# The last batch through every expert with gates instead of routing, and the tensor engine's work regrouped by tile form

## The reference, cut to what matters

```
w_eff = cos(phases) * w_real - sin(phases) * w_imag
h = conv1d(x, w_eff, taps=16)                 # 735 tokens, 64 -> 64 features
n = layernorm(h)
h = h + softmax((n Wq)(n Wk)^T / 8) n
n = layernorm(h)
logits = n gate_w + gate_b                    # 16 experts
top 2 logits, softmax over the two = two gates per token
expert e:  relu(n w1[e] + b1[e]) w2[e] + b2[e]      # 64 -> 128 -> 64
h = h + layernorm(n + sum of the two picked experts, each times its gate) * gamma + beta
```

## Time and profile before

| | |
|---|---|
| median of the runs | 450.35 us |
| the profiled execution | 450.88 us |
| its span in the trace | 449.1 us |
| PE busy | 335.5 us (75%) |
| vector engine busy | 246.3 us (55%) |
| POOL busy | 198.3 us (44%) |
| ACT busy | 127.2 us (28%) |
| mean granted TensorE clock | 0.795 of 2.4 GHz |

### The profile page before, as it was taken

One profiled execution on the slowest core, in us unless ns is written; L12 is line 12 of the kernel. 1 busy time (PEld: TensorE's weight loads), 2 busy tenths in 40 slices (PEclk: granted clock), 3 DMA queues, 4 the chain that ended last, 5 costly groups with the idle time before them and its releaser, 6 DMA issues.

```text
span 449.1 us, 6811 instructions
## 1 busy us (share of the span) xinstructions
PE 335.5 (75%) x2138; PEld 210.4 (47%) x2138; DVE 246.3 (55%) x985; ACT 127.2 (28%) x245; POOL 198.3 (44%) x241
## 2 busy tenths in 40 slices
PE   3859567868998798979897987987897776377400
PEld 1423324325654555465465445546744665266400
DVE  5357448244626584768586567848553526304305
ACT  2115103513342253235234432532142211021000
POOL 8000001710364545727572755557264726760170
PEclk9968668979698999899899989996569555555555
DMA  4970521140425241344424334323423322341110
GB/s 125 231 214 1 188 68 30 44 136 34 117 74 149 70 121 66 102 137 132 126 69 143 105 106 130 101 78 95 119 91 98 105 83 89 130 121 60 53 26 23
DMA packets 40915, 44.79 MB, mean 100 GB/s; under 512 B 11280, under 2 KB 30256, under 8 KB 40752
## 3 DMA queue, kind: packets, MB, share of 16 engines
q1 hardware_dynamic: 34736, 38.06, 27.9%
q0 software_dynamic: 6144, 6.30, 5.9%
HBM read 28.68 MB, written 15.66 MB: 99 GB/s over the span
## 4 chain that ended last, share of the span: by engine, by line
PE 62%; DVE 10%; DMA 8%; POOL 7%; ACT 7%; issue 6%; POOLq 0%; SPq 0%; ACTq 0%
PE small L962 18%; PE mix L962 14%; PE up L962 11%; PE wide L962 10%; PE mix L1138 5%; POOL x_far L470 5%; ACT hidden L574 4%; DMA xs<-x_far 2%; POOL ysel L481 2%; DVE row_max L727 2%; DMA w_far<-wt 2%; PE wide L1039 2%; PE wide L1007 1%; PE up L1079 1%; DMA x_far<-xn,place 1%
## 5 line engine op out<-in xcount | busy, mean ns | idle before, releaser
L470 POOL DMA_INDIRECT x_far<-xn,place x96 | 95.2, 992 | 166.3 <-DVE place L818 139.5
L481 POOL DMA_INDIRECT ysel<-y_far,place x96 | 93.1, 970 | 72.1 <-DMA y_far<-ys 45.0
L962 PE MATMUL small<-xt,conv_w 128*64 128x368 f32 x256 | 58.0, 577 | 12.3 <-DVE conv_w L664 7.7
L962 PE MATMUL wide<-query,keys 64*128 64x368 f32 (+2 forms) x192 | 44.0, 557 | 5.5 <-ACT query L533 5.2
L727 DVE TENSOR_REDUCE row_max<-wide 128x1 f32<-128x736 f32 (+1 forms) x48 | 43.2, 916 | 7.4 <-PE wide L962 7.4
L541 ACT ACTIVATE probs<-wide 128x736 f32<-128x736 f32 (+2 forms) x48 | 36.4, 782 | 31.5 <-PE wide L962 31.5
L962 PE MATMUL mix<-wt,hidden 128*128 128x64 f32 x256 | 41.3, 329 | 2.2 <-ACT hidden L574 2.2
L1138 PE MATMUL mix<-ident,xs 128*128 128x128 f32 x112 | 26.8, 376 | 21.1 <-DMA xs<-x_far 15.0
L962 PEld LDWEIGHTS mix<-wt,hidden 128*128 128x128 f32 x256 | 39.0, 241 | 5.8 <-issue 2.9
L574 ACT ACTIVATE hidden<-up 128x1024 f32<-128x1024 f32 (+2 forms) x32 | 24.2, 756 | 53.6 <-PE up L962 53.6
L962 PE MATMUL small<-probs,xn 128*64 128x368 f32 (+2 forms) x192 | 38.5, 499 | 0.0
(11 more groups left out here) (150 smaller groups left out, 433.6 us busy)
## 6 DMA issues: line engine op xcount, KB each, us to landing
more<-w_far SPq DMA_DIRECT2D x88, 128.0 KB, 2.2
xs<-x_far SPq DMA_DIRECT2D x24, 256.0 KB, 3.2
y_far<-ys SPq DMA_DIRECT2D x24, 256.0 KB, 2.1
xt<-x_t SPq DMA_DIRECT2D x8, 375.0 KB, 3.7
w_far<-wt SPq DMA_DIRECT2D x1, 2048.0 KB, 7.5
x_far<-xs SPq DMA_DIRECT2D x2, 864.0 KB, 6.8
wt<-w SPq DMA_DIRECT2D x3, 512.0 KB, 8.6
x_far<-xn,place POOLq DMA_INDIRECT x96
```

Source lines behind the costliest of these rows:

```text
L470: pool.indirect_dma_start(x_far[r % 2], bass.IndirectOffsetOnAxis(ap=place[r % RING][:, k:k + 1], axis=0), xn2[r % RING][:, 1, k % NT, :], ...
L481: pool.indirect_dma_start(ysel[:, k // NT, k % NT, :], None, y_far[m % 2], bass.IndirectOffsetOnAxis(ap=place[m % RING][:, k:k + 1], axis= ...
L962: return pe.matmul(dst, lhsT, rhs, start=start, stop=stop, skip_group_check=True)
```

## The change

1. **The last batch is not routed.** `routed(n)` is true for batches 0 to 6. Counting, ranking, scatter, slot loads, expert groups, gather and `combine` are gone for batch 7. In their place the vector engine spreads the two gates over 16 columns (`spread_gates`); in iteration 8 PE transposes them, ACT copies them, SP stores them to DRAM and loads each expert's 736 gates back, broadcast to 128 partitions, into the six tiles of `probs`. For each expert PE forms the hidden rows of the whole batch (`dense_up`, two products of 368 columns in 64-row form), the vector engine rectifies and multiplies by the gates in one instruction (`gate_hidden`), and PE accumulates the second layer in `small` (`dense_down`, two products of 368 columns in 64-column form). b2 enters by one small product (`dense_bias`). ACT copies the sum, three transposes bring it to tokens, and `sum_last`, `prepare`, `finish` close the batch.
2. **PE's list is regrouped** so that neighbours have the same tile form; `project(f)` comes earlier. ACT's and the vector engine's lists are reordered with it, `combine(n3)` behind the work on f.
3. **The table's steps are spread**: `table_up` before `keys_round(0)`, the constants and `table_mean` after the maxima of batch 0, `table_down` after `normalise(1)`. One more load (b2 as 16 rows) is waited for by `table_up`.
4. `cen2`, `rest` and `outs` have two buffers each.

```
@@ SP
             sp.dma_start(wt[:, :, F + D:ROW], b2 broadcast ...).then_inc(s_tab_in, 16)
+            sp.dma_start(b2s[:], b2).then_inc(s_tab_in, 16)
...
+            def load_gates(e):
+                if e >= NT:
+                    sp.wait_ge(s_dg, e - NT + 1)
+                sp.dma_start(probs[:, e % NT, :], gates_far[e].partition_broadcast(P)).then_inc(s_gin[e % NT], 16)
             def program(i):
...
-                if live(m1):
+                if routed(m1):
                     load_weights(m1, 0, 4)
+                if i == LAST_BATCH + 1:
+                    sp.wait_ge(s_gtc, 1)
+                    sp.dma_start(gates_far, gates_t[:]...).then_inc(s_gfar, 16)
+                if routed(m2):
                     store_y(m2, 2)
+                if i == LAST_BATCH + 1:
+                    sp.wait_ge(s_gfar, 16)
+                    for e in range(NT):
+                        load_gates(e)
+                if routed(m2):
                     store_y(m2, 3)
...
+                if i == LAST_BATCH + 1:
+                    for e in range(NT, E):
+                        load_gates(e)
             walk(program)
+            store(LAST_BATCH)
@@ POOL
-                if live(i - 2):
+                if routed(i - 2):
                     gather(i - 2)
-                if live(i):
+                if routed(i):
                     scatter(i)
@@ ACT, the order of program(i) after
+                if i == LAST_BATCH + 1: gates_copy()
                 shift(b); h0_copy(f); exponential(b, 0); exponential(b, 1); slots_copy(m2, 2)
-                root(0, f); exponential 2, 3; rectify(m2, 2); slots_copy(m2, 3); exponential 4, 5
-                keys_copy(f); rectify(m2, 3); attention_copy(b); query_copy(f)
+                exponential 2, 3; root(0, f); exponential 4; rectify(m2, 2); exponential 5; slots_copy(m2, 3)
+                keys_copy(f); rectify(m2, 3); query_copy(f); attention_copy(b)
                 root(2, n3); slots_copy(m1, 0); root(1, b); ...            (as before)
             walk(program)
+            mixture_copy()            # waits for all 16 dense_down
+            root(2, LAST_BATCH)
@@ vector engine
+            def gate_hidden(e):
+                dve.wait_ge(s_du, e + 1)
+                dve.wait_ge(s_gin[e % NT], 16 * (e // NT + 1))
+                if e >= HIDS:
+                    dve.wait_ge(s_dd, e - HIDS + 1)
+                dve.scalar_tensor_tensor(hid[e % HIDS][:], banks(e), 0.0, split(probs[:, e % NT, :]),
+                                         ALU.max, ALU.mult).then_inc(s_dg, 1)
             centre(0); normalise(0)
+            table_up()                # dve.wait_ge(s_tab_in, 96)
             keys_round(0); query_round(0); reduce_max(0, 0 to 5)
+            make_constants(); table_mean()
@@ vector engine, the order of program(i) after
+                centre(f); normalise(f); [i == 0: table_down()]; rectify_odd(m2, 2); combine(n3)
+                y_copy(m2, 2); keys_round(f); rectify_odd(m2, 3); prepare(n3); query_round(f); y_copy(m2, 3)
+                reduce_max(f, 0); scale_attention(b); centre_sum(b); reduce_max(f, 1); normalise_again(b)
+                reduce_max(f, 2); finish(n3); route(b); reduce_max(f, 3); y_copy(m1, 0); reduce_max(f, 4)
+                fill_tiles(b); reduce_max(f, 5); find_ranks(b); find_experts(b); find_places(b)
+                weigh_picks(b); [i == LAST_BATCH: spread_gates(b)]; y_copy(m1, 1)
+                if i == LAST_BATCH + 1:
+                    for e in range(E):
+                        gate_hidden(e)
             walk(program)
+            sum_last(LAST_BATCH); prepare(LAST_BATCH); finish(LAST_BATCH)
@@ PE
+            def dense_up(e):          # waits: gates copied (e < 2), gate_hidden(e - 3) (e >= 3)
+                for s in range(2):
+                    rows = slice(s * D, (s + 1) * D)
+                    last = mm(banks(e)[:, s, :], wt[rows, e, 0:F], x2_t[rows, 0:HALF])
+            def dense_down(e):        # waits: gate_hidden(e)
+                for s in range(2):
+                    last = mm(small[s * D:(s + 1) * D, 0:HALF], wt[:, e, F:F + D], hid[e % HIDS][:, s, :], False, False)
@@ PE, the order of program(i) after (one line for each run of one form)
+                [i == 8: transpose_gates]; transpose_max(b); to_tokens(f)
+                scores 0, 1
+                slots_to_features(m2, 2)
+                scores 2, 3
+                weigh_values 0, 1
+                first_layer(m2, 2); scores 4, 5
+                slots_to_features(m2, 3); [i == 8: dense_up(0), dense_up(1)]; second_layer(m2, 2); to_features(f)
+                weigh_values 2, 3
+                first_layer(m2, 3); project(f)
+                weigh_values 4, 5
+                second_layer(m2, 3); attention_to_tokens(b)
+                max_scores(f, 0), (f, 1)
+                convolve(c, 0, 4)
+                slots_to_features(m1, 0)
+                convolve(c, 4, 6)
+                slots_to_features(m1, 1)
+                first_layer(m1, 0); max_scores(f, 2)
+                to_features_again(b)
+                convolve(c, 6, 8)
+                max_scores(f, 3); gate_logits(b)
+                second_layer(m1, 0)
+                max_scores(f, 4); first_layer(m1, 1)
+                count_picks(b)
+                max_scores(f, 5)
+                sum_picks, rank_picks; second_layer(m1, 1); count_ends
+                if i == LAST_BATCH + 1:
+                    dense_bias(); dense_up(2)
+                    for e in range(E):
+                        dense_down(e)
+                        if e + 3 < E:
+                            dense_up(e + 3)
             walk(program)
+            dense_to_tokens()
```

More of the change, by code:

```diff
@@ L185, in build, with banks @@
         mix = ps("mix", [P, BANK])
+        def banks(e):
+            return up[:, :, 0:HALF] if e % 3 == 2 else pair(e % 3)
         def pair(k):
@@ L283, in build @@
         s_res = sem("result_ready")
+        s_gated = sem("gates_spread")
+        s_gall = sem("gates_summed")
+        s_gt = sem("gates_transposed")
+        s_gtc = sem("gates_copied")
+        s_gfar = sem("gates_in_dram")
+        s_gin = [sem(f"gates_of_expert_{k}") for k in range(NT)]
+        s_b2 = sem("b2_steps")
+        s_du = sem("dense_up")
+        s_dg = sem("dense_gated")
+        s_dd = sem("dense_down")
+        s_moec = sem("dense_copied")
+        s_moet = sem("dense_transposed")
         s_out = sem("stored")
@@ L299, in live, with routed @@
             return 0 <= n < BATCH
+        def routed(n):
+            return 0 <= n < LAST_BATCH
         @block.sync
@@ L574, in rectify, with gates_copy, mixture_copy @@
                 act.activation(hidden[:, q % 2, 0:n, 0:w], up[:, 0:n, 0:w], ACT.Relu).then_inc(s_ha, 1)
+            def gates_copy():
+                act.wait_ge(s_gt, 1)
+                copy(gates_t[:], wide[0:E, 0:2, 0:HALF]).then_inc(s_gtc, 1)
+            def mixture_copy():
+                act.wait_ge(s_dd, E)
+                copy(attn_t[:, 0:HALF], small[:, 0:HALF]).then_inc(s_moec, 1)
             act.wait_ge(s_a, 1)
@@ L594, in program @@
                     exponential(b, 1)
-                if live(m2):
+                if routed(m2):
                     slots_copy(m2, 2)
+                if live(b):
+                    exponential(b, 2)
+                    exponential(b, 3)
                 if live(f):
@@ L898, in _ @@
                 reduce_max(0, t)
+            make_constants()
+            table_mean()
             def program(i):
                 b, f, m1, m2, n3 = i, i + 1, i - 1, i - 2, i - 3
-                if live(n3):
-                    combine(n3)
                 if live(f):
                     centre(f)
+                    normalise(f)
                 if i == 0:
-                    make_table()
-                if live(f):
-                    normalise(f)
-                if live(m2):
+                    table_down()
+                if routed(m2):
                     rectify_odd(m2, 2)
-                if live(n3):
-                    prepare(n3)
-                if live(m2):
+                if routed(n3):
+                    combine(n3)
+                if routed(m2):
                     y_copy(m2, 2)
-                    rectify_odd(m2, 3)
                 if live(f):
                     keys_round(f)
-                if live(m2):
-                    y_copy(m2, 3)
-                if live(b):
-                    scale_attention(b)
+                if routed(m2):
+                    rectify_odd(m2, 3)
+                if routed(n3):
+                    prepare(n3)
                 if live(f):
                     query_round(f)
-                if live(b):
-                    centre_sum(b)
+                if routed(m2):
+                    y_copy(m2, 3)
                 if live(f):
@@ L951, in program @@
                     find_places(b)
-                if live(m1):
-                    y_copy(m1, 1)
                 if live(b):
```

(11 more changed lines are left out.)

203 lines of the change are left out of this document (130 added, 73 removed).

## The result

The changed kernel took 438.75 us (median of two runs, 438.49 and 439.02) against 450.35: ratio 0.974, 95% interval 0.970 to 0.979. It is faster, but by 11.6 us where 29 were forecast. Executions of one and the same kernel differ with the clock that they were granted (446.6 to 462.3 us for the kernel before, over 23 of them), so all ratios leave out those more than 1.5% above their kernel's fastest, while medians are over all. The span of the profiled execution is 437.3 us.

What follows compares the result with a forecast made beforehand. Middle bound by PE's list with its waits, end by latencies of one batch. 449.1 +2.5 -8 +0.6 -1.3 -22.8 = 420.1; with 1.8 outside the span and 0.5 off for the median, 421 us; range 409 to 437.

Steps and rivals of the forecast that it cites:

- Iterations 1 to 5: -8: Five full iterations: fewer switches, waits about even and fewer clock falls save 8 us; ends -15 and 0.
- So waits come out even: PE's waits per full iteration: -1.6 for old ones gone, +1.4 before second layer of group 2, +0.7 before to_features_again: +0.5.
- The clock: Low stretch per full iteration: between a fall in every one (0) and none (-1.8), the middle, -0.9 us.
- The switches: Changes of tile form on PE: 34 runs per full iteration become 25, about 0.15 us each, -1.3 us.
- Iterations 1 and 2: Iteration 1, held by slot loads, gains 0.8 us; iteration 2 loses its second low stretch, -3 us.
- Iteration 6: No convolution there, so slot loads decide, and y_copy(m2, 3) ahead of them comes later: +0.6 us.
- The opening: Start of the kernel: +2.5 us, of which +1.5 for a later first convolution and +1.0 for uncovered picks in iteration 0.
- The dense stage: From the end of second_layer(6, 1) to the span's end: 56.2 us in place of 79.0, -22.8.
- B: Rival: the clock stays at half through the experts, 13 us more, 434 us; chance 0.17.
- C: Rival: gate loads at 2.5 us each set the pace of the experts, +12, 433 us; chance 0.12.
- E: Rival: gate broadcasts take 8.9 us each, kernel slower than before, 528 us; chance 0.04 with all unseen.
- D: Rival: regrouping does nothing, each new wait brings a clock fall, ACT waits are longer; +8, 429 us; chance 0.12.

Runs made afterwards that it cites:

- e3: The changed kernel with scale_attention(b) put ahead of reduce_max(f, 0) on the vector engine; 427.95 us, ratio 0.946 to the kernel before.
- e4: e3 with ACT's slots_copy(m2, 3) and rectify(m2, 2) each put ahead of an exponential; 423.36 us, ratio 0.935 to the kernel before.
- experiment 6: The changed kernel with all table steps back in one place behind centre(1); 438.22 us, ratio 0.972 to the kernel before.
- e10: e7 with convolution steps 5 and 7 moved into the two waits behind ACT's hidden; 409.85 us, ratio 0.905 to the kernel before.
- e11: e10 with table_up behind the maxima of batch 0 instead of ahead of keys_round(0); 406.39 us, ratio 0.900 to the kernel before.
- e7: e4 with x of batch 2 loaded before SP waits for the table; 414.24 us, ratio 0.920 to the kernel before.
- e1: The kernel before with only the dense last batch and second buffers, old orders and old opening kept; 427.01 us, ratio 0.943.

## Why the prediction was wrong, point by point

**The step that failed is "Iterations 1 to 5: -8"**, and with it the range. For one of iterations 3 to 5, where the forecast was -1.4 and +3.4 came, the rows split it in three. The clock's loss is the length times one minus the mean clock; it is good to 0.2, since the clock has two digits, and it counts waits at a low clock as loss too.

| us per iteration | before | after | difference | forecast |
|---|---|---|---|---|
| waits of PE | 4.4 | 6.4 | +2.0 | +0.5 |
| loss by the clock | 0.04 x 40.95 = 1.6 | 0.12 x 44.35 = 5.3 | +3.7 | -0.9 |
| the rest | 34.9 | 32.7 | -2.2 | -1.3 |

- *The waits.* The one on `xs_t` before `second_layer(m2, 2)` came at 1.42, exactly as forecast. The one at `to_features_again` grew by 0.77, forecast 0.7. What the prediction did not see is the third, 1.64 on `attn`; nothing in it follows the vector engine's list behind `query_round(f)`: `convolve` asks for `s_attn` at L1100, and the order in the diff shows the scaling behind the maxima. "So waits come out even" left this one out.
- *The clock.* The prediction chose between one fall per iteration and none. The trace has three in iterations 4 and 5, each some 3.5 us long: behind the 1.42, behind the 1.64 and over the iteration's boundary. Iteration 3 has as much low clock, 10.2 us in all, in two: 6.8 over its beginning and 3.4 behind the 1.64, and none behind its 1.42. This is the larger error, 4.6 us per iteration. Experiment 3 puts a price on the missed wait with its clock: 2.4 us per iteration and 2.8% of the time (0.974 to 0.946).
- *The switches.* Nine fewer were priced at 1.3. The rest fell by 2.2, and it stays near 32.8 where waits and clock change: `e3` has 41.94 - 5.2 - 3.8 = 32.9, `e4` 40.31 - 4.3 - 3.2 = 32.8. So the regrouping does save work, 2.2 us per iteration, if all of the rest is put down to the forms; no run changed the forms alone with the waits as they were.
- *Iterations 1 and 2* were forecast at -0.8 and -3 and came at -1.6 and +0.7. The second low stretch of iteration 2 that was to go did not: its mean clock is 0.89, as before.
- *Iteration 6*, forecast +0.6 on the ground that the slot loads decide, came at +4.3. PE's idle time grew by 0.4 only, 7.4 to 7.8; the clock went from 0.79 to 0.68, by the same reckoning 9.0 to 15.1. It is the same error in the clock.

**What held.** The opening: the convolution of batch 2 was forecast at 61.2 and began at 61.55; `table_down` was forecast to end at 47.6 and ended at 47.9. That iteration 0 loses by the new order was forecast too, at 1.0; experiment 6 gives 2.1. The dense stage: 1.58 us per pair, no wait for a gate load once it ran, one wait on `hid` of 2.78 for "about 3". That size is luck in part: the prediction had the first hidden row wait for `finish(5)`, and 1.83 of the 2.78 was a wait for the first gate load, which it named as a sign of being wrong. The clock rose as forecast, at 386.5 and so within batch 6's groups, and a fall came too, but not at that wait: it fell near 393.5, behind a wait of 0.47 for ACT's `hidden`, 4 us earlier, and rose by 404 for the rest of the experts. The tail behind the last down: forecast 12.6, measured 12.8. The end as a whole gave 3 us more than forecast: 10.3 up to the bias product for 13.2, then 5.8 for 4.6 up to the first down, and 24.3 for 25.9 in the experts.

**The rivals.** B (half clock through the experts) fell with the 1.00 over 404 to 424; C and E (gate loads set the pace) fell with PE busy through all of those 20 us. From 399 to 405 the DMA engines moved 409 GB/s, with the gate loads in flight, which makes 0.92 us for one of 368 KB (an estimate from that rate); the forecast had 1.3. The Trainium skill ("DMA: Bandwidth & Descriptors", section Anatomy of one DMA) fits a DMA as 2.0 us and then its bytes at 436 GB/s, a fit that it gives for DMAs issued by gpsimd, which the prediction does not say. These were issued by SP, and the trace comes near that rate and has the loads hidden under PE, save the first. D came nearest to the mechanism, "every new wait brings a fall and the waits behind ACT are longer than reckoned", and sized it too small: +8 to the whole, where the middle alone had 17 and iteration 6 had 3.7. It knew neither the wait on `attn` nor the fall at the iteration's end. The margin of the range above 421 was made from B, C and D at these sizes, and so ended 1.75 us short.

**What stays open.** What decides at which wait the clock falls. It is not the list alone: in one execution of `e10` iterations 3 and 4 run the same list in 37.9 and 41.0 us, at 0.95 and 0.87. Nor is it the list with its waits: iteration 4 of `e10` (low from 182.5 to 189.5 and again from 220.5 on) and iteration 3 of `e11` (1.00) have nearly the same waits, within 0.3 us each and none over 0.72. What the runs show is narrower: in the profiles with waits of 1.05 to 1.64 left in the list the clock fell in each of iterations 3 to 5, and with all of them below 0.8 it held for 143 us in `e11`, though not in `e10`. What filling the 1.22 alone would do is not known either: a version of `e7` with idle products there (`e8`) gave no result, since they need a tile of PSUM to write to, and nothing kept ACT from still reading the one that they were given.

## What to carry to other kernels

When a list is reordered, write down for every instruction of the busiest engine which function of the other engines it waits for, and look for that function's new place in *its* list; a two-line swap on the vector engine was worth 2.8% here, where the regrouping alone had cost 1.6% (0.5% to 2.7%). Price short waits not at their length alone but with the clock: here an iteration with waits of about 1 us and more had 3.4 to 10.2 us at half rate, and taking one wait away moved part of that to the next one. A saving in switches counts only once the waits that it makes are gone: nearly the same regrouped list ran an iteration in 44.35 us with them and, in its best execution, in 37.2 without. And look at more than one execution before a low stretch is put down to the wait ahead of it.

## What the runs showed of the hardware that was not expected

- In iterations 4 and 5 of the changed kernel a wait of 1.42 us or 1.64 us was followed by about 3.5 us at 0.50 of 2.4 GHz, that is at 1.2 GHz, although PE was fully busy again (3.00 of 3.00 in both rows above). It is not so behind every such wait: not behind the 1.42 of iteration 3, nor behind those of iterations 3 to 5 of `e1`. The low stretches of an iteration cost more (5.3) than all that the regrouping saved (2.2).
- Waits of 0.72 us and less can go with a low clock too: in `e10` it was at 0.50 for some 7 us from 182.5 on. Filling one wait of 1.42 with work (`e5`) brought no gain (1.013, 1.002 to 1.024).
- Broadcasts of 368 KB, up to six in flight, landed a median of 5.2 us after issue, with 409 GB/s moved from 399 to 405. The first, issued with five others behind it, took 5.9 and held up the vector engine for 1.83; the later ones kept up with PE at 1.58 us per expert, while the 512 KB broadcast in pieces of 256 bytes had needed 12.4.
